# The last group's routing spread over more tiles, its tables in four pieces, its scatters in smaller lumps

## What is computed

```python
scores = jax.nn.softmax(xt @ gate_w.T, axis=-1)
biased = scores + gate_b
_, idx = jax.lax.top_k(biased, TOPK)                      # TOPK = 2, E = 8
weights = jnp.take_along_axis(scores, idx, axis=-1)
...
h = swiglu((xt @ ew1 + eb1) * (xt @ ew3 + eb3))           # for each expert
acc + ce[:, None] * (h @ ew2 + eb2)                       # ce: weight of the token for the expert
```

## Time and profile before

| | |
|---|---|
| median of 3 runs (range) | 423.24 us (423.03 to 425.62) |
| the profiled execution, its own time | 423.07 us |
| its span, first to last instruction | 421.3 us |
| outside the span | 1.8 us |
| mean granted TensorE clock | 0.960 of full |
| busy: TensorE, VectorE, ScalarE, GpSimd | 347.6, 281.5, 175.3, 194.0 us |
| the tile part | from about 238 to 397 us of the span |

### The profile page before, as it was taken

The page is one execution under the profiler, slowest core; times in us unless marked ns, Lnnn a source line. Parts: engine busy times, 40 slices in busy tenths (PEclk is TensorE's granted clock), DMA queues, the critical chain, the costliest instruction groups (busy, mean ns, idle before and its releaser), DMA issues.

```text
span 421.3 us, 8518 instructions
## 1 busy us (share of the span) xinstructions
PE 347.6 (82%) x2415; PEld 224.6 (53%) x2415; DVE 281.5 (67%) x834; ACT 175.3 (42%) x498; POOL 194.0 (46%) x377
## 2 busy tenths in 40 slices
PE   2637887888988879798967998978799999999880
PEld 1224466666656658576656554534455555555450
DVE  3435477777878897869876867987466666666322
ACT  2212344444534443344532344344355555555313
POOL 9700022224222558722474434357755656565323
PEclk9999999998999998969998799999899999999996
DMA  4764544766654732310003001113211111110063
GB/s 100 171 212 128 178 141 120 210 202 172 186 157 132 201 98 63 104 34 11 27 28 119 14 13 44 33 39 92 63 45 44 47 45 45 40 50 19 26 201 100
DMA packets 53197, 39.56 MB, mean 94 GB/s; under 512 B 7623, under 2 KB 46632, under 8 KB 53147
## 3 DMA queue, kind: packets, MB, share of 16 engines
q1 hardware_dynamic: 50881, 34.33, 29.3%
q0 software_dynamic: 2272, 4.69, 3.3%
HBM read 26.05 MB, written 12.69 MB: 92 GB/s over the span
## 4 chain that ended last, share of the span: by engine, by line
PE 42%; DVE 23%; issue 10%; POOL 9%; DMA 6%; SPq 5%; ACT 2%; ACTq 0%; POOLq 0%; DVEq 0%
PE pT L1491 7%; PE pS L1491 6%; DVE negmax L934 4%; PE pM L1502 4%; POOL xs L633 3%; PE pM L1297 3%; DVE inv_den L950 2%; POOL rstd L613 2%; PE pO L1482 2%; PE pT L1321 2%; PE pT L1492 2%; PE pS L1311 2%; PE pS L1492 2%; PE pO L1334 2%; DVE X L1004 1%
## 5 line engine op out<-in xcount | busy, mean ns | idle before, releaser
L711 POOL DMA_INDIRECT ys<-sim_rhs,row_dest x39 | 40.5, 1039 | 43.3 <-ACT sim_rhs L868 41.7
L766 ACT ACTIVATE PT<-pT 128x512 f32<-128x512 f32 x64 | 38.0, 594 | 33.3 <-PE pT L1321 29.9
L1491 PE MATMUL pT<-W,XH 128*128 (+1 forms) x94 | 51.7, 632 | 0.0
L934 DVE TENSOR_REDUCE negmax<-pS 128x4 f32<-128x512 f32 x64 | 43.4, 679 | 9.6 <-PE pS L1311 9.2
L1071 DVE TENSOR_TENSOR PT<-pT,PT 128x512 f32<-128x512 f32 x47 | 32.4, 689 | 25.9 <-PE pT L1492 17.7
L1491 PE MATMUL pS<-W,XH 128*128 (+1 forms) x94 | 49.3, 607 | 0.0
L611 POOL TENSOR_SCALAR vareps<-meanvar 128x1 f32<-128x1 f32 x32 | 8.4, 263 | 86.1 <-DVE meanvar L963 85.8
L1311 PE MATMUL pS<-Kdiag,Qst 128*128 128x512 f32 x64 | 40.4, 638 | 6.3 <-DMA Kdiag<-parts_scr 4.7
L852 ACT COPY XH<-pO 128x384 f32<-128x384 f32 x47 | 22.4, 478 | 49.4 <-PE pO L1484 45.7
L1502 PEld LDWEIGHTS pM<-W,XH 128*128 128x128 f32 x188 | 28.1, 191 | 21.0 <-issue 17.4
L633 POOL DMA_INDIRECT xs<-X,slot x32 | 33.2, 1036 | 8.1 <-issue 5.8
(11 more groups left out here) (264 smaller groups left out, 828.1 us busy)
## 6 DMA issues: line engine op xcount, KB each, us to landing
parts_scr<-qk_hi SPq DMA_DIRECT2D x16, 256.0 KB, 2.9
W<-in_L_ffn_w SPq DMA_DIRECT2D x16, 256.0 KB, 3.9
Qst<-parts_scr SPq DMA_DIRECT2D x32, 96.0 KB
Kdiag<-parts_scr SPq DMA_DIRECT2D x64, 48.0 KB
Kst<-parts_scr SPq DMA_DIRECT2D x32, 96.0 KB
Qdiag<-parts_scr SPq DMA_DIRECT2D x64, 48.0 KB
sim_add<-xs SPq DMA_DIRECT2D x39, 65.0 KB
parts_scr<-qk_lo SPq DMA_DIRECT2D x8, 256.0 KB, 3.0
```

Source lines behind the costliest of these rows:

```text
L711: pool.indirect_dma_start(ys.ap(), bass.IndirectOffsetOnAxis(ap=row_dest[:, k:k + 1], axis=0), YO[:, i % RING, :], None).then_inc(s_ysc[i ...
L766: act.activation(PT[:, u % 3, :], pT[:, 0, :], ACT.Exp, scale=SCALE).then_inc(p_sb, 1)
L934: dve.tensor_reduce(out=negmax[:, b % 2, HG * j:HG * (j + 1)], in_=pS[:, u % 2, :].rearrange("p (g k) -> p g k", g=HG), axis=AX.X, op=ALU.max,
L1491: pe.matmul(bank, XH[:, 1 - p, 2 * P:3 * P], W[:, bass.ds(e_up * I2, I2)], start=True, stop=False)
```

## The change

Group 3's nine routing steps stood ahead of six tiles (m = 6 to 11) and now stand ahead of eight (m = 6 to 13): one step to a tile, only steps 4 and 5 share one. `late_tiles` is cut into `late_counts` (five instructions) and the rest (six), `tile_table` into `tile_experts` (three) and `tile_rows` (four); the four pieces stand ahead of the tiles at m = 14, 15, 16 and 17, where the two whole ones stood at 12 and 13. The counting matmuls go from m = 10 to 11. SyncE's zeros go from behind load(9) to behind load(11). GpSimd's eight scatters stand behind place(3) to place(8), in lumps of 2, 1, 1, 2, 1, 1. The number of instructions is the same.

```diff
-PAD_LOAD = 9
-LAST_ROUTING = {6: (0,), 7: (1, 2), 8: (3, 4), 9: (5,), 10: (6, 7), 11: (8,)}
-LAST_COUNT, LAST_TILES, LAST_TABLE = 10, 12, 13
+PAD_LOAD = 11
+LAST_ROUTING = {6: (0,), 7: (1,), 8: (2,), 9: (3,), 10: (4, 5), 11: (6,), 12: (7,), 13: (8,)}
+LAST_COUNT, LAST_TILES = 11, 14
+LAST_SCATTER = {3: (0, 1), 4: (2,), 5: (3,), 6: (4, 5), 7: (6,), 8: (7,)}
...
                 place(i)
                 if i + RING < NR:
                     meta(i + RING)
-                if i in (1, 3):
-                    for k in range(G4):
-                        scatter(NG - 1, (i // 2) * G4 + k)
+                for k in LAST_SCATTER.get(i, ()):
+                    scatter(NG - 1, k)
...
                 if m == LAST_TILES:
+                    late_counts()
+                if m == LAST_TILES + 1:
                     late_tiles()
-                if m == LAST_TABLE:
-                    tile_table(NE, NR - NE)
+                if m == LAST_TILES + 2:
+                    tile_experts(NE, NR - NE)
+                if m == LAST_TILES + 3:
+                    tile_rows(NE, NR - NE)
                 tile(m - 1, (m - 1) % 2)
```

More of the change, by code:

```diff
@@ L1172, in early_tiles, with late_counts, late_tiles @@
                 link(dve.tensor_tensor(step[:], start[:, 1:E + 1], start[:, 0:E], ALU.subtract))
-            def late_tiles():
+            def late_counts():
                 round_tiles((P - 1) / (2.0 * P))
                 link(dve.tensor_tensor(tiles[:], tiles[:], used[:], ALU.subtract))
+            def late_tiles():
                 first_tiles()
@@ L1180, in late_tiles, with tile_experts @@
                 link(dve.tensor_tensor(step[:], start[:, 1:E + 1], start[:, 0:E], ALU.subtract))
-            def tile_table(first, n):
+            def tile_experts(first, n):
                 link(dve.tensor_tensor(past[:, 0:n], iota_t[:, 0:n].rearrange("p (t o) -> p t o", o=1).to_broadcast([1, n, E]),
@@ L1188, in tile_table, with tile_rows @@
                 link(dve.tensor_scalar(expert_of[:, NA + first:NA + first + n], tab_f[:, 0:n], float(E - 1), None, ALU.min))
+            def tile_rows(first, n):
                 link(dve.tensor_tensor(past_step[:, 0:n], past[:, 0:n], bass.AP(step, 0, [[E, 1], [0, n], [1, E]]), ALU.mult))
@@ L1246, in _ @@
                 if n == EARLY_TILES + 1:
-                    tile_table(0, NE)
+                    tile_experts(0, NE)
+                    tile_rows(0, NE)
                 if n >= FFN_SLOT + 1:
```

## The result

The changed kernel takes 417.50 us (median of 6 runs, 415.0 to 419.23), the kernel before 423.73 in its 6 runs with it (423.03 to 425.62): ratio 0.984, interval 0.980 to 0.988. So it is 6.2 us faster; 416.9 was predicted.

A forecast was written before the change was run, and what follows sets the result against it. Before tile 19 VectorE, without gaps, keeps TensorE waiting, plus a halt; afterwards TensorE's 3.034 us beat bounds. 1.9 + 4.4 - 0.2 = 6.1 us off 423.07 gave 416.9 us; the 8-in-10 range was 415.3 to 422.3.

The forecast's parts named there:

- Part 1: Routing and tables ahead of VectorE's tiles: spreading them lets TensorE idle less, 1.9 us gained (ends 0.9 and 2.9).
- The chain of VectorE's starts: Each VectorE tile begins 2.29 us plus its extra work after the last; TensorE starts 2.47 us later, two tiles on.
- Part 2: GpSimd's later scatters: the last at 306.9 us, rows usable 5.13 later, before tile 23 needs them; no cost.
- The 1.6 us of cover: Margin before tile 23: load(16) has the last scatter's rows at 312.0 us, needed at 313.6.
- Part 3: Spaced scatters remove the halt behind the second lump: 0 to 4.44 us, upper end taken, called the shakiest choice.
- the halt: Unexplained stop of TensorE, VectorE and ScalarE between tiles 17 and 19, behind the second lump of four scatters; 4.44 us lost.
- a rival ("the lumps are not what stopped them"): The halt stays since scatter lumps don't cause it; only 1.9 us gained, 421.2 us; chance 0.24.
- Part 4: SyncE's zeros behind load(11): load(12) usable at 300.1 to 301.9 us, tile 19 needs 301.5; cost 0.2 us.
- The rival that they hold up tile 19: Zeros beside the scatters delay load(12), so tile 19 waits up to 3.4 us; 419.7 to 421.4 us, chance 0.11.
- The halves of the sum: Gains from spreading routing and tables, 1.9 us, and from removing the halt, 4.4 us.

The follow-up runs named there:

- lumps_only: Kernel before with only the scatters respaced as in the change (lumps of 2, 1, 1, 2, 1, 1); ratio 0.994 to the kernel before.
- routing_only: Changed kernel with the scatters in two lumps of four again, behind place(3) and place(5); ratio 0.996 to the kernel before.
- one_to_a_place: Changed kernel with the eight scatters one behind each of place(3) to place(10); ratio 1.013 to the kernel before.
- zeros_spread: Kernel before with the eight zero blocks one behind each of load(8) to load(15); ratio 1.003 to the kernel before.
- finer_tables: Changed kernel with the tables in six pieces ahead of VectorE's tiles 13 to 18 instead of four; ratio 0.985 to the kernel before.
- before_again: The kernel before, unchanged, profiled once more in one execution; tiles 7 to 19 took 46.8 us, against 46.4 in its first trace.

## Why the prediction was right

**Part 1, 1.9 us.** The chain of VectorE's starts had tile 19 at 40.0 us behind tile 7; it came at 40.1. Term by term: VectorE's tiles 9 to 16 were foreseen at 273.2, 276.1, 279.5, 282.6, 285.9, 289.4, 292.6, 296.0 and came, less the 1.45 of the front part, at 273.05, 276.13, 279.53, 282.56, 285.89, 289.37, 292.60, 296.01. Tile 17 was foreseen at 295.1 and came at 296.55 - 1.45 = 295.1. That the routing and the scatters each account for part of it is shown by the two halves: 3.7 us (lumps_only) and 3.6 (routing_only, to tile 24) of 6.3. How they add up isn't settled: in the traces they make 7.3, more than the whole, and in the timed ratios 2.6 + 1.8 = 4.4, less than the whole's 6.7.

**Part 2.** Last scatter foreseen at 306.9, came at 309.12 - 1.45 = 307.7, and its 5.13 us to the first tile was confirmed by one_to_a_place. The 1.6 us of cover was really 0.9 (tile 23 starts at 315.14).

**Part 3, the upper end of 0 to 4.44.** The choice was called the shakiest and held; lumps_only shows it in the profile. Its reason was half right. The lumps do make the halt, but what in them does, length or rate, is open, and the words on a lump "beside SyncE's blocks" were wrong twice: the eight blocks (282.51 to 292.43) ran beside the first lump, behind which there is hardly a halt, and ended as the second began; and zeros_spread left the halt as it was. That the full 4.44 came off was luck in part: the rows before gave no way to know that the change's spacing was wide enough, nor that the chip would be one on which the halt comes. What stops the engines is not found. The rule of the Trainium skill's page "SBUF — State Buffer", section "SBUF: two separate sides", that TensorE and ScalarE never wait on anyone for SBUF, isn't contradicted, since nothing shows the halt to be at a memory port. Its use as a rival ("the lumps are not what stopped them") is: the kernels that differ in the placing of scatters alone differ in the halt.

**Part 4, 0.2 us for the zeros.** Foreseen pitch 1.12 to 1.37, measured (289.99 to 299.79 for seven) 1.40, yet load(12) was issued only 0.47 us behind the last block, not 1.85, so nothing was lost where 0.2 had been put. The rival that they hold up tile 19 came true in routing_only, at 0.71 us, and in finer_tables, at 0.54.

**The halves of the sum.** 1.9 and 4.4 fit the profile of the first chip. On the third chip only the first half seems to be there to win.

## What to carry to other kernels

When two engines alternate, add up for each tile the slack of the one behind and cut side work to pieces that fit into it; a chain of starts, with one sum for each engine, told this kernel's starts to 0.15 us. Before moving work later, write down the last moment at which each consumer must have it: here 3.8 us more on the last scatter turned the gain into a loss. In these traces close rows of indirect DMAs from GpSimd beside a busy TensorE came with a halt on each of the three chips on which they were traced, and spaced ones with little or none; where a trace has idle times that no releaser explains, try spacing them among the engine's other work, and measure on more than one chip.

## What was not expected of the hardware

- The halt concerns TensorE's signals. In the semaphore events of both traces of the kernel before, the releases of four TensorE steps of tiles 16 and 17, which the modelled ends put 2.5 us apart, come within 0.15 us: 300.49, 300.54, 300.59, 300.64 and 302.71, 302.76, 302.81, 302.86. ScalarE and VectorE start right behind them. Three such releases within 0.17 us stand between 296 and 303 us in lumps_only, routing_only and zeros_spread too, and none in that stretch of the changed kernel. Whether the matmuls or only their releases were held back stays open.
- The spread of one kernel's runs, 1% for the changed kernel, comes in good part from the front part: tile 7 started between 261.08 and 263.86 us in fourteen traces, though no edit touches what it waits for. In before_again it starts 1.8 us later than in the first trace of the same kernel, and the span is 2.3 longer.
- A wait of 2.87 us of TensorE cost 5.8, because the tile behind it then ran at the lower clock (a granted 0.51 over 317 to 323 us) and took 2.96 us more.
